# A fused attention and feed-forward kernel: another order of issue for the first three groups of its second attention

## What is computed

```python
x = x + _L0_xattn_ref(_layernorm(x), ctx, ctx, ...)   # gated linear attention, 8 heads
x = x + _L0_ffn_ref(_layernorm(x), ...)               # 8 experts, the best 2 of each token, and a shared one
x = x + _L1_xattn_ref(_layernorm(x), ctx, ctx, Wq, bq, Wk, bk, Wv, bv, Wp, bp)
x = x + _L1_ffn_ref(_layernorm(x), w1, w3, w2)

# _L1_xattn_ref, H = 16, HD = 8
q = _split_heads(query @ Wq.T + bq)
k = _split_heads(key @ Wk.T + bk)
v = _split_heads(value @ Wv.T + bv)
score = jnp.einsum('bhqd,bhkd->bhqk', q, k) * SCALE
attn = jax.nn.softmax(score, axis=-1)
out = jnp.einsum('bhqk,bhkd->bhqd', attn, v)
return merge_heads(out) @ Wp.T + bp
```

## Time and profile before

| | us |
|---|---|
| median of 3 runs | 1101.4 |
| lowest and highest | 1099.48, 1102.79 |
| the profiled execution | 1100.62 |
| its span | 1098.8 |
| attention's first transfers to the end of the first peaks (in the span) | 639 to 677 |
| attention's loop | 680 to 956 |

### The profile page before, as it was taken

One profiled execution on the slowest core, in us unless ns is written; L12 is line 12 of the kernel. 1 busy time (PEld: TensorE's weight loads), 2 busy tenths in 40 slices (PEclk: granted clock), 3 DMA queues, 4 the chain that ended last, 5 costly groups with the idle time before them and its releaser, 6 DMA issues. The chain is left out here.

```text
span 1098.8 us, 24814 instructions
## 1 busy us (share of the span) xinstructions
PE 902.1 (82%) x9121; PEld 644.6 (59%) x9121; DVE 734.4 (67%) x2271; ACT 534.6 (49%) x848; POOL 505.7 (46%) x566
## 2 busy tenths in 40 slices
PE   5820988875887776699999915899999999899997
PEld 1210666653555554466666613788888888666665
DVE  6753588887776766287887746777777775255553
ACT  2423676753433333276666632556656665232321
POOL 4300146656777677055555556765665630011110
PEclk9965999996888897799999968999999999899999
DMA  8524444425123223524333221121111310123431
GB/s 246 211 66 128 111 145 133 139 62 193 46 71 81 68 71 95 152 87 125 117 121 123 95 79 37 40 55 42 54 50 41 100 50 12 49 60 101 116 78 38
DMA packets 84742, 101.35 MB, mean 92 GB/s; under 512 B 36144, under 2 KB 57456, under 8 KB 83856
## 3 DMA queue, kind: packets, MB, share of 16 engines
q1 hardware_dynamic: 55088, 77.88, 23.3%
q0 software_dynamic: 8192, 16.79, 5.3%
q10 hardware_dynamic: 21344, 5.12, 2.7%
HBM read 64.88 MB, written 30.67 MB: 87 GB/s over the span
## 5 line engine op out<-in xcount | busy, mean ns | idle before, releaser
L1006 POOL TENSOR_TENSOR moe_h_lo<-moe_hid,moe_h_hi 128x512 f16<-128x512 f32 x78 | 90.6, 1162 | 103.6 <-ACT moe_h_hi L1159 98.6
L1685 ACT ACTIVATE split_table<-attn_psT 128x1024 f32<-128x1024 f32 x64 | 65.6, 1025 | 100.2 <-PE attn_psT L1564 100.2
L1153 ACT ACTIVATE moe_act_g<-moe_psG,split_unscale 128x512 f32<-128x512 f32 x110 | 75.5, 687 | 71.1 <-PE moe_psU L1088 40.0
L1263 DVE SCALAR_TENSOR_TENSOR moe_hid<-moe_psU,split_to_hidden,moe_act_g 128x512 f32<-128x512 f32 x110 | 80.9, 747 | 38.9 <-ACT moe_act_g L1153 38.8
L1748 DVE TENSOR_REDUCE split_table<-attn_psN 128x16 f32<-128x1024 f32 x62 | 75.5, 1218 | 12.3 <-PE attn_psN L1539 12.0
L1159 ACT ACTIVATE moe_h_hi<-moe_hid 128x512 f16<-128x512 f32 x110 | 68.3, 621 | 31.5 <-DVE moe_hid L1263 28.7
L1000 POOL DMA_INDIRECT scratch_xs<-cell_xn,res_row x64 | 62.4, 976 | 29.1 <-issue 18.2
L1000 POOL DMA_INDIRECT scratch_xs<-moe_xn,res_row x64 | 62.3, 973 | 24.2 <-issue 18.7
L285 POOL TENSOR_SCALAR ffn_shifted<-ffn_mv 128x4 f32<-128x4 f32 x16 | 3.7, 229 | 148.4 <-DVE ffn_mv L266 117.7
L1481 POOL DMA_INDIRECT cell_h<-scratch_ys,res_slot x64 | 62.2, 972 | 20.8 <-issue 20.8
L1576 PE MATMUL attn_psO<-heads_vheads,split_table 128*64 128x18 f32 x2048 | 71.3, 212 | 0.1
(11 more groups left out here) (277 smaller groups left out, 2660.2 us busy)
## 6 DMA issues: line engine op xcount, KB each, us to landing
mlstm_vals<-in_values SPq DMA_DIRECT2D x16, 544.0 KB, 3.7
mlstm_keys<-in_keys SPq DMA_DIRECT2D x16, 512.0 KB, 3.6
scratch_ys<-cell_h SPq DMA_DIRECT2D x26, 256.0 KB, 2.0
res_x<-in_x SPq DMA_DIRECT2D x16, 256.0 KB, 6.1
early_ctxT<-in_ctxT SPq DMA_DIRECT2D x16, 256.0 KB, 6.4
attn_in_ctxT<-attn_in_ctxT ACTq DMA_DIRECT2D x64, 64.0 KB
scratch_x<-split_table SPq DMA_DIRECT2D x16, 256.0 KB, 2.3
out<-raw_keys SPq DMA_DIRECT2D x32, 128.0 KB, 2.3
```

The lines of the kernel that those rows point to most:

```text
L1006: pool.tensor_tensor(h_lo[u % 3][c][:, :], hid[u % 2][c][:, :], h_hi[u % 3][c][:, :], ALU.subtract).then_inc(lo_done[c], 1)
L1153: act.activation(act_g[c][:, :], psG[c][:, :], ACT.Silu, scale=sw.unscale[:, 0:1]).then_inc(silu_done, 1)
L1263: v.scalar_tensor_tensor(out=hid[u % 2][c][:, :], in0=psU[c][:, :], scalar=sw.to_hidden[:, 0:1], in1=act_g[c][:, :], op0=ALU.mult, op1=ALU ...
L1685: act.activation(probT[i % 2][:, :, :, :, :].rearrange("p r b m q -> p (r b m q)"), psT[:, :], ACT.Exp).then_inc(prob_done, 1)
```

## The change

Groups 0, 1 and 2 get another order ahead of the loop, and the loop starts with group 1 instead of group 0 on TensorE, ScalarE and VectorE. GpSimd and SyncE keep their orders. No instruction is added or taken away; some are moved.

- TensorE: the four `plain` of group 0 stand together, then its `turn_peak` and first `scores`; `turn(1)` and `q_(1)` come behind these, between the scores of group 0. The loop's first round is written out, with `values(0, i)` ahead of the scores that follow.
- VectorE: `peak_of(0, 0)` stands ahead of `statistics(1)`, and `normalise(1)` between the third and the fourth peak. `combine(2)` stands behind `heads_out(0, 0)`, `peak_of(1, 0)` ahead of `statistics(2)`, `combine(3)` behind `normalise(2)` and ahead of `peak_of(1, 3)`.
- ScalarE: `probs(0, 0)` stands ahead of `xnT_out(1)`, and so on by the order of TensorE.
- Two waits are fitted to it: `turn_peak(0)` waits for the queries of group 0 in place of those of group 1, and `turn(1)` for the shift of group 0.

```diff
@@ turn
-                if g >= 2:
-                    pe.wait_ge(shift_done, ONE + g - 1)
+                    pe.wait_ge(shift_done, ONE + max(g - 1, 1))
@@ turn_peak
-                pe.wait_ge(q_done, ONE + min(g + 2, GROUPS))
+                pe.wait_ge(q_done, ONE + (min(g + 2, GROUPS) if g else 1))
@@ TensorE, behind q_(0)
-            plain(0, 0)
-            plain(0, 1)
+            for i in range(TILES):
+                plain(0, i)
+            turn_peak(0)
+            pe.wait_ge(sel_in, ONE + 16)
+            scores(0, 0)
             turn(1)
-            plain(0, 2)
-            plain(0, 3)
+            scores(0, 1)
             q_(1)
-            turn_peak(0)
+            values(0, 0)
+            scores(0, 2)
             plain(1, 0)
+            values(0, 1)
+            scores(0, 3)
             plain(1, 1)
-            pe.wait_ge(sel_in, ONE + 16)
-            for g in range(LAST):
+            values(0, 2)
+            plain(1, 2)
+            turn(2)
+            plain(1, 3)
+            q_(2)
+            plain(2, 0)
+            turn_peak(1)
+            plain(2, 1)
+            for g in range(1, LAST):
@@ ScalarE, behind v_out(1)
-            for g in range(2):
-                xnT_out(g)
-                q_out(g)
-            for g in range(LAST):
+            xnT_out(0)
+            q_out(0)
+            probs(0, 0)
+            xnT_out(1)
+            probs(0, 1)
+            q_out(1)
+            probs(0, 2)
+            k_out(2)
+            probs(0, 3)
+            xnT_out(2)
+            q_out(2)
+            v_out(2)
+            for g in range(1, LAST):
@@ VectorE, behind combine(1)
+            peak_of(0, 0)
             statistics(1)
-            peak_of(0, 0)
+            peak_of(0, 1)
+            peak_of(0, 2)
             normalise(1)
-            for i in range(1, TILES):
-                peak_of(0, i)
+            peak_of(0, 3)
             split_peak(0)
             shift_out(0)
+            heads_out(0, 0)
+            combine(2)
             peak_of(1, 0)
-            combine(2)
             statistics(2)
+            heads_out(0, 1)
+            peak_of(1, 1)
+            heads_out(0, 2)
+            peak_of(1, 2)
             normalise(2)
-            for g in range(LAST):
+            combine(3)
+            peak_of(1, 3)
+            split_peak(1)
+            statistics(3)
+            peak_of(2, 0)
+            shift_out(1)
+            normalise(3)
+            for g in range(1, LAST):
```

## The result

The changed kernel takes 1109.33 us in the median of 6 runs (1104.42 to 1112.07), the kernel before beside it 1101.72; the ratio is 1.0059 with a 95% interval of 1.0037 to 1.0081. Forecast was 1102.3 in a range of 1099.4 to 1105.3: the time lies above it, and the change is slower by more than 0.3%.

What follows compares the result with a forecast made beforehand. TensorE was taken to bound attention once its loop is filled, so only the start of `plain(2, 3)` counted: +0.9 us, through a later `combine(2)` and the gathers behind it, on a median of 1101.4 gave 1102.3 us, range 1099.4 to 1105.3.

## What to carry to other kernels

When a reordering opens a gap on TensorE in a filling phase, price the work behind that gap at half clock for 3 to 14 us, the span seen here, and not for the shortest stretch of one profile; one profile is one sample of it. Where the order allows it, keep independent work in such a gap (as the kernel before has the turn and projection of the next group) instead of behind it, and do not queue the start of a long chain, as `combine(2)` here, behind a wait on another engine when its data have landed.

## What the runs showed of the hardware

- The granted clock stayed at 0.50 (1.2 GHz) for 12 us in which TensorE was busy for 12.00 of 12. In another profile of the same kernel the later part of the same work (from `values(0, 3)` on) ran at 0.99. What decides it isn't shown by these runs.
- A gap of 2.40 us was harmless in the kernel before, and behind one of 1.96 us in the changed kernel the clock was at 1.00. In gaps of 2.56, 2.35 and 1.76 us the clock fell, 2.3, 1.0 and 0.5 us after TensorE had stopped, and stayed down for 10.2, 6.8 and 13.6 us; behind gaps of 2.56, 2.34 and 2.72 us in another execution of that kernel it was down for 6.8, 3.4 and 6.8 us.
- Beside a block of 3.74 us on GpSimd four operations of VectorE took 3.12 us instead of 1.14, and beside one of 2.49 us 1.99.
- Code that is the same began attention anywhere from 639.5 to 644.2 us in fourteen profiles.
